# The end of a linear-attention stage reordered over two units, and the last sums of a routed FFN taken by halves

## The reference

```python
qkv = silu(einsum('bnf,of->bno', h, w_qkv))                 # h: normed x
# blocks of 32 with a carried state; equal to: o = (q k^T * decay, causal) v, per head
out = norm_w * (out * rsqrt(mean(out * out, -1) + EPS))     # over all heads
attn = einsum('bno,fo->bnf', sigmoid(h @ w_gate.T) * out, w_out)
x = x + ga * attn
h = layernorm(x) * (1 + cb) + sb
logits = h @ gate_w.T;  scores = softmax(logits);  topk_w, topk_idx = top_k(scores, 2)
moe = sum over e of cw[:, e] * (silu(g_e) * u_e @ w2_e)     # g_e, u_e = split(h @ w1_e)
x = x + gb * (moe + shared(h))
```

## Time and profile before

| | |
|---|---|
| median of 3 runs | 1194.93 us (1194.69 to 1197.26) |
| profiled execution | 1193.11 us |
| span in its trace | 1191.2 us |
| PE busy | 1073.6 us, 90% of the span |
| VectorE busy | 916.4 us, 77% |
| ScalarE busy | 735.7 us, 62% |
| GpSimd busy | 343.3 us, 29% |

### The profile page before, as it was taken

The page is one execution under the profiler, slowest core; times in us unless marked ns, Lnnn a source line. Parts: engine busy times, 40 slices in busy tenths (PEclk is TensorE's granted clock), DMA queues, the critical chain, the costliest instruction groups (busy, mean ns, idle before and its releaser), DMA issues. The chain is left out here.

```text
span 1191.2 us, 21657 instructions
## 1 busy us (share of the span) xinstructions
PE 1073.6 (90%) x7276; PEld 919.8 (77%) x7276; DVE 916.4 (77%) x1850; ACT 735.7 (62%) x1389; POOL 343.3 (29%) x353
## 2 busy tenths in 40 slices
PE   5879787768999999999999999999999987769995
PEld 4645555546889899989998999899989976659993
DVE  6688889847778778778788788788787776787775
ACT  5668686756666566666665666666666653635650
POOL 3376454453311101110111111101111333863440
PEclk8789798979999999999999999999999996899998
DMA  7210000119304003003003003012000001444426
GB/s 276 68 45 10 15 6 15 41 43 90 86 3 123 10 10 116 9 9 116 9 9 116 9 10 115 9 38 86 9 18 27 1 1 42 131 151 117 125 91 220
DMA packets 62325, 72.16 MB, mean 61 GB/s; under 512 B 21841, under 2 KB 49617, under 8 KB 61234
## 3 DMA queue, kind: packets, MB, share of 16 engines
q1 hardware_dynamic: 58850, 61.90, 19.3%
q0 software_dynamic: 3408, 9.39, 2.1%
HBM read 36.39 MB, written 32.78 MB: 58 GB/s over the span
## 5 line engine op out<-in xcount | busy, mean ns | idle before, releaser
L1447 PE MATMUL attn_psum<-all_h_parts,attn_wp 128*128 128x512 f32 x1152 | 300.7, 396 | 0.0
L1447 PEld LDWEIGHTS attn_psum<-all_h_parts,attn_wp 128*128 128x128 f32 x1152 | 211.1, 188 | 40.8
L1602 ACT CAST attn_pp<-attn_p 128x512 fp32r<-128x512 f32 (+3 forms) x256 | 117.3, 458 | 199.4 <-DVE attn_p L1696 197.3
L1827 POOL TENSOR_TENSOR all_gate<-all_gate,attn_sq 128x512 f32<-128x512 f32 x64 | 84.6, 1321 | 502.1 <-ACT attn_sq L1613 502.0
L1677 DVE TENSOR_TENSOR attn_pp<-attn_p,attn_pp 128x512 fp32r<-128x512 f32 (+3 forms) x256 | 198.8, 777 | 8.1 <-ACT attn_pp L1602 8.1
L1526 PE MATMUL attn_psum<-attn_qkp 128*128 128x512 f32 (+3 forms) x768 | 164.4, 323 | 4.5 <-DVE attn_qkp L1677 4.5
L1473 PE MATMUL attn_psum<-attn_pp,attn_vp 128*128 128x512 f32 (+3 forms) x768 | 162.9, 321 | 0.8 <-issue 0.4
L1473 PEld LDWEIGHTS attn_psum<-attn_pp,attn_vp 128*128 128x128 f32 x768 | 129.0, 189 | 21.2 <-issue 1.3
L1526 PEld LDWEIGHTS attn_psum<-attn_qkp 128*128 128x128 f32 x768 | 125.1, 189 | 13.1 <-DVE attn_qkp L1677 3.0
L1696 DVE TENSOR_TENSOR attn_p<-attn_psum,attn_mask 128x512 f32<-128x512 f32 (+3 forms) x256 | 123.8, 484 | 4.9 <-PE attn_psum L1526 3.7
L983 DVE TENSOR_REDUCE front_top<-front_psum 128x2 f32<-128x256 f32 (+3 forms) x128 | 100.9, 816 | 25.8 <-PE front_psum L644 25.7
(11 more groups left out here) (368 smaller groups left out, 1834.4 us busy)
## 6 DMA issues: line engine op xcount, KB each, us to landing
expert_rows<-attn_empty SPq DMA_DIRECT2D x8, 2080.0 KB, 10.3
all_wraw<-in_w1p SPq DMA_DIRECT2D x8, 1024.0 KB, 5.1
all_yacc<-expert_rows SPq DMA_DIRECT2D x39, 130.5 KB, 2.2
attn_mask<-decay_masks SPq DMA_DIRECT2D x16, 256.0 KB, 2.6
experts_wx<-expert_results SPq DMA_DIRECT2D x6, 512.0 KB, 8.6
experts_xraw<-in_wx SPq DMA_DIRECT2D x4, 608.0 KB, 4.1
all_wraw<-in_wx SPq DMA_DIRECT2D x4, 608.0 KB, 4.0
all_x<-in_x SPq DMA_DIRECT2D x4, 512.0 KB, 7.4
```

Source lines behind the costliest of these rows:

```text
L1447: last = nc.tensor.matmul(out, wp[:, a, k, col:col + P], hh[:, c, k, b * S:(b + 1) * S], start=(m == 0), stop=(m == 5))
L1602: nc.scalar.copy(pp[:, u % 2, 0, cols], p[:, cols]).then_inc(p_hi, 1)
L1827: nc.gpsimd.tensor_tensor(cols, cols, sq[:, h, :], ALU.add).then_inc(summed, 1)
```

## The change

It has four edits. In the second attention, last pair only:

1. On ScalarE the cast of the normed batch 0 (`scalar_high`, 128x1024) moves from the end of unit 6 behind the third scores block of unit 7, and the scaling of batch 1 (`scalar_scale`, four operations) from the end of unit 6 behind `finish_unit(5)` in unit 7.
2. On VectorE the low part of batch 0 (`vector_low`) moves from the middle of unit 7 to behind the last `y_low`. `gate_unit(6)` moves into unit 7, ahead of its last `scores_low`, and the two `add_output` of unit 7 move behind `y_low(6)`.
3. The last output of PE, 24 matmuls as before, is ordered by head: the 12 of head 0 wait for `y_low(6)`, the 12 of head 1 for `y_low(7)`.

At the end of the experts:

4. Batch 2 is summed by VectorE alone, as the parts before it. PE sums batch 3 only, and signals each half of it; VectorE takes the halves one by one.

```diff
@@ tensor, behind the last values() @@
-                pe.wait_ge(y_ready, PAIRS * UNITS)
                 pe.wait_ge(y_added, PAIRS * 2 * B - 2)
-                for i in range(2):
-                    output(("y", 1, i))
+                for h in range(2):
+                    pe.wait_ge(y_ready, PAIRS * UNITS - 1 + h)
+                    for i in range(2):
+                        for half in range(2):
+                            tt = 2 * i + half
+                            for m, (a, c) in enumerate(TERMS):
+                                last = nc.tensor.matmul(ps[:, Y_BANK + i, half * D:(half + 1) * D],
+                                                        yp[:, a, h, tt * P:(tt + 1) * P], wop[:, c, h, :],
+                                                        start=(h == 0 and half == 0 and m == 0),
+                                                        stop=(h == 1 and half == 1 and m == 2))
+                        if h == 1:
+                            last.then_inc(y_full, 1)
@@ scalar body @@
                         if late(it, u, 2):
                             finish_unit(u - 2, it)
+                        if last_pair and u == NEXT_AT + 1:
+                            late_norm.scalar_scale(nc, act, 1, 1)
...
                         scores_hi(u, 2, it)
+                        if last_pair and u == TURN_AT + 1:
+                            late_norm.scalar_high(nc, act, 0, 0)
...
                             for k in range(KT):
                                 late_norm.scalar_ht(nc, act, 0, 0, k, Y_BANK + k)
-                            late_norm.scalar_high(nc, act, 0, 0)
-                        if last_pair and u == NEXT_AT:
-                            late_norm.scalar_scale(nc, act, 1, 1)
@@ vector body @@
-                        if last_pair and u == TURN_AT + 1:
-                            late_norm.vector_low(nc, dve, 0, 0)
...
-                            add_output(u, 0, it, first)
+                            if last_pair and u == UNITS - 1:
+                                gate_unit(u - 1, it)
+                            else:
+                                add_output(u, 0, it, first)
                         scores_low(u, 3, it)
...
-                        elif late(it, u, 3):
+                        elif late(it, u, 3) and not (last_pair and u == UNITS - 1):
                             add_output(u, 1, it, first)
@@ vector, behind the body @@
-                for u in (UNITS - 2, UNITS - 1):
-                    gate_unit(u, PAIRS - 1)
-                    y_low(u, PAIRS - 1)
+                y_low(UNITS - 2, PAIRS - 1)
+                for i in range(2):
+                    add_output(UNITS - 1, i, PAIRS - 1)
+                gate_unit(UNITS - 1, PAIRS - 1)
+                y_low(UNITS - 1, PAIRS - 1)
+                late_norm.vector_low(nc, dve, 0, 0)
                 late_norm.vector_stats(nc, dve, 1, 1)
@@ experts, tensor @@
-                for b in (2, B - 1):
-                    pe.wait_ge(results_in[b + 1], 32)
-                    for half in range(2):
...
+                pe.wait_ge(results_in[B], 32)
+                for half in range(2):
+                    for c in range(2):
+                        tt = (B - 1) * TB + 2 * half
...
                     last.then_inc(pair_made, 1)
@@ experts, vector @@
-                for i, part in enumerate(PARTS[:3]):
+                for i, part in enumerate(PARTS[:4]):
...
+                for half in range(2):
+                    part = slice((B - 1) * TB + 2 * half, (B - 1) * TB + 2 * half + 2)
+                    dve.wait_ge(pair_made, half + 1)
+                    nc.vector.tensor_tensor(upd[:, 2 * half:2 * half + 2, :],
+                                            ps[:, Y_BANK + half, :].rearrange("p (t n) -> p t n", t=2),
+                                            t["gate"][:, 3, B - 1:B, :].to_broadcast([P, 2, D]), ALU.mult).then_inc(y_gated, 1)
+                    dve.wait_ge(y_gated, 5 + half)
+                    nc.vector.tensor_tensor(x[:, part, :], x[:, part, :], upd[:, 2 * half:2 * half + 2, :], ALU.add
+                                            ).then_inc(x_final, 1)
```

More of the change, by code:

```diff
@@ L2489, in _ @@
                 down(LATE + 1)
-                for b in (2, B - 1):
-                    pe.wait_ge(results_in[b + 1], 32)
-                    for half in range(2):
-                        for c in range(2):
-                            tt = b * TB + 2 * half
-                            last = nc.tensor.matmul(bank((Y_BANK if b == B - 1 else T_BANK) + half), t["ident"][:, :],
-                                                    results[:, c, tt:tt + 2, :].rearrange("p t n -> p (t n)"),
-                                                    start=(b == 2 and c == 0), stop=(c == 1))
+                pe.wait_ge(results_in[B], 32)
+                for half in range(2):
+                    for c in range(2):
+                        tt = (B - 1) * TB + 2 * half
+                        last = nc.tensor.matmul(bank(Y_BANK + half), t["ident"][:, :],
+                                                results[:, c, tt:tt + 2, :].rearrange("p t n -> p (t n)"),
+                                                start=False, stop=(c == 1))
                     last.then_inc(pair_made, 1)
@@ L2786, in _ @@
                     nc.vector.tensor_tensor(xb, xb, y, ALU.add).then_inc(x_final, 1)
-                for i, (b, at_bank) in enumerate(((2, T_BANK), (B - 1, Y_BANK))):
-                    dve.wait_ge(pair_made, i + 1)
-                    if i:
-                        dve.wait_ge(x_final, 4)
-                    nc.vector.tensor_tensor(upd.rearrange("p (i t) n -> p i t n", t=2),
-                                            ps[:, at_bank:at_bank + 2, :].rearrange("p i (t n) -> p i t n", t=2),
-                                            t["gate"][:, 3, b:b + 1, :].unsqueeze(1).to_broadcast([P, 2, 2, D]),
-                                            ALU.mult).then_inc(y_gated, 1)
-                    dve.wait_ge(y_gated, 4 + i)
-                    if b == 2:
-                        nc.vector.tensor_tensor(x[:, rows(b), :], x[:, rows(b), :], upd, ALU.add).then_inc(x_final, 1)
-                    else:
-                        for half in range(2):
-                            part = slice(b * TB + 2 * half, b * TB + 2 * half + 2)
-                            nc.vector.tensor_tensor(x[:, part, :], x[:, part, :], upd[:, 2 * half:2 * half + 2, :], ALU.add
-                                                    ).then_inc(x_final, 1)
+                for half in range(2):
[7 more added lines that the diff above has]
+                                            ).then_inc(x_final, 1)
             @block.gpsimd
```

## The result

| | before | changed |
|---|---|---|
| median, 20 runs of each | 1197.63 us | 1190.97 us |
| profiled execution | 1193.11 us | 1190.32 us |
| span in its trace | 1191.2 us | 1188.5 us |

What follows compares the result with a forecast made beforehand. Taken as bounds: the second attention's late y_low with PE's output behind it, and the last sums' identity matmuls. Gains of 3.5 and 1.6 us, 5.1 together, off the median 1194.93 gave 1189.8 us, range 1188.5 to 1191.2.

Steps and rivals of the forecast that it cites:

- Part 1, ScalarE's order: Unit 7: ScalarE casts scores (7,0) 2.56 us earlier, so y_low(5) and PE's output follow; GpSimd's wide operations 2.2 us earlier.
- Part 2, VectorE's order: End of second attention: y_low(7) 3.1 us earlier, moved low part 2.2 us at its new place, layer norm 3.5 us earlier.
- Part 3, PE's order: PE's last attention output: split by heads it ends 0.9 us before VectorE asks; unsplit it would cost about 1 us.
- Part 4, the last sums: End of experts: PE's eight passes on batch 3 take 5.2 us from the landing; x ready 1.6 us earlier.
- The cold tail: End of kernel: clock rises only after PE's 8 passes, 6.9 us, so the tail gives nothing; 1191.4 us; 12%.
- A worse collision with GpSimd: Unit 7: one more hold of VectorE, about 1.9 us on the path, leaves 1.6 of 3.5; 1191.7 us; 15%.
- more than summed: Low-clock stretch between tail's work and routing falls away, or moved low part not held: 2 us more; 1187.8 us; 13%.
- slower tiles: Expert loop: PE idle longer beforehand keeps first tiles at the low level, 1.7 us more a tile; 1198.3 us; 3%.

Runs made afterwards that it cites:

- low_back: Changed kernel with batch 0's wide low part and its cast back at their old places; unit 5's gating to last layer norm 21.02 us, against 21.00.
- best: Changed kernel with the edits of gate_first and warm; ratio 0.9894 to the kernel before, median 1182.86 us.
- warm: Changed kernel with 11 unread matmuls on PE ahead of its wait for batch 3; first result-transfer issue to last addition 20.32 us, 2.15 less.
- adds_back: Changed kernel with unit 7's two additions back ahead of unit 6's gating; unit 5's gating to last layer norm 21.28 us, against 21.00.
- act_only: Kernel before with ScalarE's order changed and nothing else; unit 5's gating to last layer norm 22.26 us, 2.9 less than before.
- gate_first: As stats_first, with unit 7's gating also ahead of its two additions; unit 5's gating to last layer norm 19.26 us, against 21.00.
- stats_first: Changed kernel with batch 1's statistics ahead of batch 0's wide low part; unit 5's gating to last layer norm 19.64 us, against 21.00.

## Why the prediction was right, step by step

- *Part 1, ScalarE's order: right.* y_low(5) comes 2.55 us after the start of A instead of 5.06: 2.51 us earlier, where 2.56 was forecast. The runs bear the step out: undone, it costs 2.85 us; alone, it brings the last y_low 2.3 us forward. The slide of GpSimd's two wide operations came, and was made up for: the first waits 0.29 us for the scaling (976.23) and starts 2.2 us earlier, as forecast, but it then takes 2.51 us instead of 2.82, so the second ends 9.86 us after the start of A instead of 12.36, 2.5 earlier and not 2.2.
- *Part 2, VectorE's order: the sum is right in its pieces, and one of them was not needed.* Block 2's low part ends 3.64 us earlier (3.2 forecast), the last gating starts 3.75 earlier (3.1), the statistics 1.52 (0.8), and the norm 4.14 (3.5). About 0.3 of the missing 0.6 is GpSimd's earlier end. The moved low part took 2.31 us, with 2.2 forecast. The step also had the hold right: it let the low part of block 2 wait for GpSimd in its place, so it counts only 1.1 us for the wide one in the middle and 2.2 at the end. What it never asks is whether that exchange gains anything. low_back shows that it doesn't: 1.1 us for the low part and 0.9 for its high part in the middle stand against 2.31 at the end. The expectation for low_back missed because it let the low part put back what follows by some 2.5 us instead of 1.1.
- *Part 3, PE's order: right.* No wait of the additions for PE, with a cover of 1.4 us (0.9 forecast), since PE started earlier and the clock rose 2.9 us into the 24 matmuls. The size for the low level is a misreading: the 5.13 us of before are not all at 0.50, since the clock rose 4.6 us into them. All 24 at 0.50 took 5.49 us in best, so the forecast cover was 0.5 us and not 0.9, and in the changed kernel 0.3 would have been left. The price of both heads waited for at once was 0.6 us and not 1, in an execution with the clock low for nearly all of PE's output; that PE's order is needed, as the part says, isn't shown for an earlier rise.
- *Part 4, the last sums: right in this execution.* PE started 15.57 us after the first issue (15.8 forecast), took 5.44 us (5.2), and T fell by 1.57 us (1.6). The sizes hang on the clock's rise, which came 3.4 to 5.8 us after PE's start over the nine executions with this tail in which it began low, and 2.9 to 5.1 us over three with the old one. (The text expected of warm gives these times for its six traces as 3.9 to 6.3; the windows show 3.4 to 5.8.) The mean T of the nine is 23.1 us and of the three 24.6, so the averages differ by 1.5, close to the forecast's 1.6.
- *The rivals.* The cold tail has its mechanism right: in adds_back the rise came at 5.8 us, the 8 passes took 6.56 and T was 24.43, no less than before. It is a matter of single executions, and old tails have it too (25.64 in act_only). A worse collision with GpSimd did not come: in the middle of unit 7 VectorE is held at the same three places as before, and the one new hold, at the end, was in the sum. The rival "more than summed" said 7.1 us, and as a ratio, 1187.8 / 1194.93 = 0.9940, it is nearer to the measured 0.9939 than the forecast is. In the trace only 0.6 us of its 2 is found, in A, and neither of the causes named for it was at work: the moved low part was held, and the stretch from the barrier to the tail is no shorter. Of slower tiles nothing is seen: from the experts' first matmul to the first issue of results the traces show 168.04 us before and 168.34 after.
- *What stays open.* The two stretches give 5.7 us in the trace, and the two halves timed apart give 5.1. The whole change gave 7.3 us, and 8.2 in the second timing. The intervals reach down to 5.5 and 5.3, so nothing is contradicted, but both lie on the same side. By the medians the whole change gave 6.7 and 6.2 us, and the two halves 4.5 and 1.9, so part of the gap is how runs are averaged. The stretch of the experts varied between 166.0 and 170.9 us over all 14 traces, and the time up to A between 968.0 and 973.9, in no order that goes with an edit. The experts' stretch took 168.0 to 168.2 us in the three traces with VectorE's old order and 168.3 on average in the other eleven, so no hidden gain is seen there. Whether the change has a share in the rest wasn't found. It is the same with best: its A and T are 4.8 and 3.2 us shorter, 8.0 together, and its interval begins at 9.6. Its trace is of the second longest of its six executions (1186.14 us); with the A of gate_first and the T of warm it would be 9.6.

## What to carry to other kernels

Look, on every engine, for work that is read late and queued ahead of a small operation that the others wait for: putting two such pieces back costs 2.85 of 4.1 us here. When an operation is long because it is held by another engine, don't count its whole time as the gain of moving it: ask whether the next one inherits the hold, and whether an operation that isn't held can stand there instead. And where a short piece of PE work behind a long idle time ends the kernel, the clock's rise decides its length; here 11 matmuls that nobody reads kept it from falling, and the last 8 passes took 3.70 us instead of 5.4 to 6.6.

## What the hardware showed

- *Which operations of VectorE are held beside GpSimd.* Those with two inputs in SBUF were: 0.69 us became 1.78, 0.41 became 1.73, 1.20 became 2.31. The statistics with one input took 1.40 us beside a GpSimd sum, against 1.39 behind it, and a mask product of 128x384 with one input in PSUM took 0.55 at 976.41, under a wide GpSimd operation, against 0.54 at 882.14 in the kernel before, with GpSimd idle.
- *GpSimd can be the one that waits.* A small operation of 0.23 us took 1.11 beside the wide low part in stats_first, and a sum of 1.28 us took 1.71 in gate_first, where the last y_low had started 0.11 us ahead of it.
- *The rise of the clock after idleness is no constant.* The same tail, after an idle time of 9.3 to 11.0 us, saw it 3.4 to 5.8 us after PE's start, worth up to 1.2 us of PE time (5.38 to 6.56 us for eight passes); with PE kept busy, in warm and best, it stood at 1.00 through the tail, and the eight took 3.70 us.
